# One block of scores per attention step, expert tiles in two phases, a prologue of two chains and the logits on GpSimd, in an attention and mixture-of-experts kernel on one core

## The reference, cut to what matters

```python
h = relu(patches(x, 5 frames) @ tok_W.T + tok_b)       # [32, 121, 128]
h = batch_norm(h) * gamma + beta                       # statistics over all 3872 rows
# attention in each sequence, with one bias per head and key column
xn = layernorm(h)
q, k, v = (xn @ w.T + b for each of q, k, v)           # heads of 16
scores = q @ k.T / 4 + col_bias                        # [32, 8, 121, 121]
h = h + softmax(scores) @ v @ o_w.T + o_b
# one expert per row
xf = layernorm(h)
expert = argmax(xf @ Wr + br)                          # top 1, its gate is 1
h = h + relu(xf @ W1[expert] + b1[expert]) @ W2[expert] + b2[expert]
```

## Time and profile before

| stretch of the profiled execution | us | what happens |
|---|---|---|
| 0 to 43.9 | 43.9 | prologue, up to the first scores |
| 43.9 to 206.8 | 162.9 | the starts of steps 0 to 31 |
| 206.8 to 242.5 | 35.7 | step 31, emptying, the table of tiles, first load |
| 242.5 to 313.6 | 71.1 | 38 expert tiles on PE |
| 313.6 to 326.6 | 13.0 | last rows out, end of the program |

### The profile page before, as it was taken

How to read it: one execution, slowest core, us unless ns; L and a number is a source line. 1 busy time by engine, 2 the same in 40 slices (tenths; PEclk the granted TensorE clock), 3 DMA queues, 4 the chain that set the end, 5 groups by cost and what they waited for, 6 DMA issues and landing times.

```text
span 326.6 us, 9082 instructions
## 1 busy us (share of the span) xinstructions
PE 256.3 (78%) x2851; PEld 211.5 (65%) x2851; DVE 193.1 (59%) x754; ACT 165.2 (51%) x427; POOL 140.7 (43%) x256
## 2 busy tenths in 40 slices
PE   3896577988898887789788978674149999999970
PEld 3765455765676665666556757442139999999970
DVE  3796325656766766757667657744716556656640
ACT  3761145655545555465555443421027777777730
POOL 7002621233426644564556363355603445545550
PEclk9995579999979999889999799955559999999996
DMA  3200698000000001001010101112133333333300
GB/s 99 67 2 0 197 314 252 3 2 0 3 17 17 25 25 33 17 18 33 15 34 17 33 16 36 31 32 57 56 87 90 94 104 117 93 107 101 87 11 0
DMA packets 15373, 19.13 MB, mean 59 GB/s; under 512 B 4007, under 2 KB 11467, under 8 KB 15328
## 3 DMA queue, kind: packets, MB, share of 16 engines
q1 hardware_dynamic: 11888, 12.15, 13.3%
q0 software_dynamic: 3296, 6.00, 6.2%
q10 hardware_dynamic: 144, 0.41, 0.4%
HBM read 10.58 MB, written 8.47 MB: 58 GB/s over the span
## 4 chain that ended last, share of the span: by engine, by line
PE 41%; issue 23%; POOL 20%; DVE 7%; ACT 4%; DMA 1%; POOLq 1%; SPq 1%; DVEq 0%; ACTq 0%
PE psS L1091 11%; POOL region_d L375 6%; PE psO L1102 5%; PE psU L1102 5%; POOL rs L347 3%; POOL rs L369 3%; PE psU L1028 2%; PE psS L928 2%; DVE sq L640 2%; PE psB L912 2%; ACT PT L492 2%; POOL var L364 2%; PE psU L1038 2%; POOL rows L358 2%; POOL xn L353 1%
## 5 line engine op out<-in xcount | busy, mean ns | idle before, releaser
L728 DVE TENSOR_REDUCE nmax<-psS 121x4 f32<-121x484 f32 x64 | 41.5, 660 | 41.7 <-PE psS L938 21.5
L403 POOL DMA_INDIRECT out<-y_out,sidx x38 | 36.9, 972 | 45.8 <-DVE y_out L832 42.2
L841 DVE TENSOR_SCALAR hT<-psS,b1T 128x128 f32<-128x128 f32 x76 | 23.3, 346 | 34.3 <-PE psS L1091 34.0
L1091 PE MATMUL psS<-xgT,W_tile 128*128 128x128 f32 x304 | 41.9, 283 | 0.0
L375 POOL DMA_INDIRECT region_d<-rows,pos x32 | 34.7, 1083 | 9.5 <-issue 8.7
L1091 PEld LDWEIGHTS psS<-xgT,W_tile 128*128 128x128 f32 x304 | 38.6, 199 | 0.0
L484 ACT ACTIVATE rows<-rows,rs 121x128 f32<-121x128 f32 x32 | 12.9, 402 | 48.1 <-POOL rs L369 48.0
L1028 PE MATMUL psU<-owX,oT 128*121 128x137 f32 x64 | 16.6, 344 | 21.3 <-ACT oT L495 21.3
L928 PE MATMUL psS<-kT,qT 32*121 32x121 f32 x512 | 23.7, 301 | 10.6 <-DVE kT L666 8.6
L541 ACT ACTIVATE hT<-psS,b1T 128x128 f32<-128x128 f32 x76 | 23.8, 364 | 14.1 <-PE psS L1091 14.0
L928 PEld LDWEIGHTS psS<-kT,qT 32*121 32x121 f32 x512 | 18.0, 190 | 18.9 <-issue 18.9
(11 more groups left out here) (223 smaller groups left out, 608.3 us busy)
## 6 DMA issues: line engine op xcount, KB each, us to landing
xg<-region_d SPq DMA_DIRECT2D x38, 129.0 KB, 2.1
W_sb<-in_L_ffn_W SPq DMA_DIRECT2D x1, 2048.0 KB, 9.2
region_d<-pads SPq DMA_DIRECT2D x1, 1032.0 KB, 7.0
region_d<-pads SPq DMA_DIRECT2D x1, 903.0 KB, 9.1
out<-y_out,sidx POOLq DMA_INDIRECT x38, 2.2
...
region_d<-rows,pos POOLq DMA_INDIRECT x32
...
```

Of the source, the lines that this page charges most:

```text
L403: pool.indirect_dma_start(out, bass.IndirectOffsetOnAxis(sidx[:, s:s + 1], 0), y_out[:, u, :], None, bounds_check=N - 1, oob_is_err=False) ...
L728: dve.tensor_reduce(nmax[0:L, pair * 64:pair * 64 + 64].rearrange("p (j c) -> p j c", c=HB)[:, :, HD + 1:HD + 3], score_half(0, pair), AX. ...
L841: ins = dve.tensor_scalar(hT[:, s % 2, c * 128:(c + 1) * 128], psS[:, 2 + s % 2, c % 2 * 128:(c % 2 + 1) * 128], b1T[:, bass.ds(e * FC + c ...
L1091: ins = pe.matmul(psS[:, c // 2 * 2 + s % 2, c % 2 * 128:(c % 2 + 1) * 128], W1_tile[:, s % 2, c * 128:(c + 1) * 128], xgT[:, s % 2, :], s ...
```

## The change

- **One block per step.** `nmax` is one instruction over all four banks, and so is the exponent. The order in a step is now maxima of t first, and then the exponent of t - 1, which waits for them.
- **Order of the queues.** On ACT the copy of the turned result (`turned_copy`) stands at the front of a step, and the scaling of the rows of t - 5 (`scaled_rows`) at its end. On DVE K's copy stands ahead of `qm`. On PE the output multiplication no longer has an exponent ahead of the ACT copy that it waits for.
- **Logits on Pool.** Instead of one DVE instruction per sequence, POOL does two instructions for each group of four. `rs2` has eight slots, so the wait on the scaling of b - 4 becomes one on b - 8.
- **Groups.** All groups have four sequences (8 groups). Their row bases are carried in `seen`, which takes one matmul out of each ranking.
- **Two phases of tiles.** After five groups (`EARLY`, sequences 0 to 19) the rows are counted in step 27 (`COUNT`), and the first NT1 = 11 full tiles are placed by step 29. SP loads them as soon as the rows of 20 sequences have landed. Their processing starts in the emptying: steps 32 to 36 each hold one tile (`ALONG` = 5). Tiles 5 to 10 follow, while DVE works out the table of the remaining NT2 = 27 tiles, one tile slot per partition. These 27 follow as before. In the first phase the output of W2 goes to one buffer in `psB` and not to two. The ring of row buffers has 12 instead of 8 places.
- **Prologue.** The identity matrix is made first, and PE starts on the patches with only that and `xs`. The one-hot rows are 64 `tensor_scalar` instructions of 121 columns, all ahead of the `bn_stats`. Half of their matmuls stand ahead of the frame multiplication, and half behind. ACT makes the copies of the weights and the first squares. K of the first pair is projected before the bias is turned, and Q after it. The third pair's turning stands behind these projections, and the second pair's norm is turned inside step 0.

The diff, cut to its core:

```diff
-RING = 8
+RING = 12
-XT = NT - -(-N // 128)
+EARLY = 5
-GROUPS = tuple((b, 4) for b in range(0, B - 8, 4)) + tuple((b, 2) for b in range(B - 8, B, 2))
+GROUPS = tuple((b, 4) for b in range(0, B, 4))
+B1 = GROUPS[EARLY - 1][0] + GROUPS[EARLY - 1][1]
+NT1 = (B1 * L - E * 127 + 127) // 128
+NT2 = NT - NT1
-        STEPS = B + 6
+        STEPS = B + 5
-            return b0 + nb + 5
+            return b0 + nb + (5 if b0 + nb <= B - 8 else 6 if b0 + nb < B else 4)
+        COUNT = ranked(EARLY - 1) + 2
+        ALONG = STEPS - B
...
-            sp.wait_ge(d_rows, 16 * B)
-            sp.wait_ge(d_pads, 32)
             sp.wait_ge(r_row, 1)
-            for s in range(NT):
+            first = first_row(0)
+            sp.wait_ge(d_early, 16 * B1)
+            sp.wait_ge(d_pads, 16)
+            load_rows(0, first)
+            for s in range(1, NT1):
+                load_rows(s, first_row(s))
+            sp.wait_ge(r_row, 2)
+            first = first_row(NT1)
+            sp.wait_ge(d_rows, 16 * (B - B1))
...
+            def logits(g):
...
+                pool.wait_ge(s_r2, b0 + nb)
+                pool.tensor_tensor(lg[0:L, v:v + nb, :], rows[0:L, b0:b0 + nb, 0:E],
+                                   rs2[0:L, v:v + nb].unsqueeze(2).to_broadcast([L, nb, E]), ALU.mult).then_inc(s_lg, 1)
+                pool.wait_ge(s_lg, 2 * g + 1)
+                pool.tensor_tensor(lg[0:L, v:v + nb, :], lg[0:L, v:v + nb, :],
+                                   br_bc[0:L, :].unsqueeze(1).to_broadcast([L, nb, E]), ALU.add).then_inc(s_lg, 1)
...
+            def exponent(b):
+
+                act.wait_ge(s_ST, b + 1)
+                if b + 1 < B:
+                    act.wait_ge(s_max, b + 2)
+                if b >= 2:
+                    act.wait_ge(s_PV, b - 1)
+                act.activation(PT[0:L, b % 2, :, :, :], score_half(1), ACT.Exp).then_inc(s_exp, 1)
...
-                dve.tensor_tensor(target1h[:, 8 * c:8 * c + 8, :],
-                                  slot_iota[:, 1:L + 1].unsqueeze(1).to_broadcast([128, 8, L]),
-                                  keyT[:, 8 * c:8 * c + 8].unsqueeze(2).to_broadcast([128, 8, L]),
-                                  ALU.is_equal).then_inc(a_1h, 1)
+            for c in range(8):
+                for f in range(8 * c, 8 * c + 8):
+                    ins = dve.tensor_scalar(target1h[:, f, :], slot_iota[:, 1:L + 1], keyT[:, f:f + 1], None, ALU.is_equal)
+                ins.then_inc(a_1h, 1)
...
-                    for pair in range(2):
-                        if pair == 1 and t > 0:
-                            dve.wait_ge(s_exp, 2 * t - 1)
-                        dve.tensor_reduce(nmax[0:L, pair * 64:pair * 64 + 64].rearrange("p (j c) -> p j c", c=HB)[:, :, HD + 1:HD + 3],
-                                          score_half(0, pair), AX.X, ALU.max, negate=True).then_inc(s_max, 1)
+                dve.tensor_reduce(nmax[0:L, :].rearrange("p (j c) -> p j c", c=HB)[:, :, HD + 1:HD + 3], score_half(0),
+                                  AX.X, ALU.max, negate=True).then_inc(s_max, 1)
...
+            for t in range(B + 1, STEPS):
+                s = t - B
+                e = tile_expert(s - 1)
...
+                if has(t, 3):
+                    turn_back(t - 3)
...
+                if has(t, 4):
+                    output(t - 4)
+                if has(t, 2):
+                    weigh(t - 2)
+                pe.wait_ge(f_xT, s + 1)
+                transpose_rows(s + 1)
+                ffn_first(s)
...
+                    turn(t - 3)
...
+                ffn_second(s - 1, e)
```

979 lines of the change are left out of this document (601 added, 378 removed).

## The result

The changed kernel takes **266.48 us** (median of four runs from 264.37 to 267.29), beside 327.67 us for the kernel before on the same chip: ratio 0.8119, 95% interval 0.8067 to 0.817. The profiled execution took 264.37 us by its own time, with a span of 262.6 us.

A forecast was written before the change was run, and what follows sets the result against it. PE was taken to bound the experts, latency the emptying, and a ring of waits to cost the nearly PE-full attention steps 0.82 us each. Gains of 17 + 5.5 + 16 = 38.5 us gave 289 us, range 277 to 303.

The forecast's parts named there:

- That is 4.43 us of work in a step of 5.25 us: Attention steps before the change: PE busy 137.4 of 162.9 us over 31 step starts, its busy time taken as work.
- The forecast of 4.7: Attention steps: the time in us taken for one step after the change, down from 5.25.
- The 5.0: Attention steps: upper bound in us of a step, if only the `oT` wait goes and a third of it returns.
- The ring: Attention steps: DVE's squares, POOL's root, ACT's scaling, exponent, DVE's second maxima; said to lose PE 0.82 us a step.
- part 1: Attention steps: reordered queues shorten 31 steps from 5.25 to 4.70 us, gaining 17 us, between 8 and 25.
- The cover of 3.0 us: Attention steps: PE work between one `scores_T` and the next scores, said to hide 2.5 us of maxima and exponent.
- PE full: Rival, attention steps: steps come down to 4.45 us, part 1 gives 25 us, time 281 us; chance 0.2.
- Another wait takes its place: Rival, attention steps: maxima or K's copy hold steps at 5.0 us, part 1 gives 8, time 298 us; chance 0.2.
- POOL becomes the bound: Rival, attention steps: the logits stretch POOL until steps exceed 5.95 us and the kernel is slower; chance 0.02.
- Part 2, 5.5 us: Prologue: statistics 2 us sooner, PE's earlier start 0.5, fetch to first scores 3; gain 5.5 us, between 3 and 7.
- Part 3: Emptying and experts: tiles begun in the emptying and a second phase gain 16 us, between 10 and 21.
- The tail: Program end: last row scatter starts 4.4 us after PE's end and 8.6 us follow, expected unchanged.

## Why the prediction was off

**The step that failed: "That is 4.43 us of work in a step of 5.25 us".** PE's busy time was taken for its work, and so for the least that a step can take. It is not work alone. The trace of before has one even step without a wait, step 4, the last one without a scaling. Here it is beside a step with the clock low and the two steps of the earlier trace rows (columns of the earlier trace rows):

```profile
60.81:65.17 4.36, 4.36 (x67) 3.60 (x67) 2.91 (x13) 2.77 (x8) 0.39 (x2) 1.00 0.02 6
92.51:98.44 5.93, 5.93 (x66) 5.03 (x66) 3.63 (x17) 2.75 (x8) 2.25 (x5) 0.71 0.09 24
148.51:153.72 5.21, 4.81 (x67) 3.64 (x67) 3.65 (x17) 2.95 (x9) 2.24 (x5) 1.00 0.10 28
153.72:159.79 6.07, 4.47 (x67) 3.33 (x67) 4.61 (x19) 3.25 (x9) 3.81 (x7) 1.00 0.08 21
```

The same 67 matmuls at the same clock are busy for 4.36 us without waits and for 4.81 with them. A matmul is recorded with 0.26 to 0.29 us, though in a block the next one starts 0.03 us later, so the first tenths of a stop do not show as idle. Step 20 has an example:

```profile
151.36 0.49 PE L1028 MATMUL psU<-owX,oT 128*121 128x137 f32 x2 [0.36 <-ACT oT L495]
151.90 0.32 PE L1038 MATMUL psU<-ident,nmax 121*128 121x121 f32 x1
```

The second maxima end at 151.84, and PE's turning of them starts at 151.90, 0.54 us after the block ahead of it, where 0.24 is enough in the timeline of the changed kernel. No idle time stands there. The steps 20 and 21 hold 9.29 us of busy time; an even step and an odd one with a ranking take PE 4.34 + 3.93 = 8.27 us now (with one bf16 matmul fewer). The least could thus have been read from the trace of before: 4.36 us in step 4, or from start to start of PE's blocks wherever no wait stands. In the changed kernel's timeline the ten gaps are 0.53, 0.53, 0.16, 0.22, 0.44, 0.46, 0.24, 0.19, 0.56 and 1.01 us, or 4.34. The clock has a small part too: the three even steps of before with a granted clock of 0.71 to 0.72 took 5.93, 5.87 and 5.30 us where the others took 5.0 to 5.2, some 1.5 us together, all booked as busy, and the changed kernel has none of them.

The forecast of 4.7, chosen between 4.43 and 5.0, was thus between two numbers that were both too high. The 5.0 does not follow from its own terms either: 5.25 less two thirds of 0.69 is 4.8.

**The ring was read rightly in the main.** The two moves that the first paragraph of part 1 names, scaling and K's copy, make 32.1 of the 37.6 us in the kernel before. But "the exponent no longer waits for POOL" was only half of it. With the maxima in one piece, the copy to `oT` is the edge that costs (13.0 us if it is behind the scaling, 0.5 if only the exponent is). The cover of 3.0 us of PE's work for maxima and exponent was enough: ACT waits 15.2 us for `nmax`, and PE hardly at all for ACT.

**The rivals.** "PE full" (0.2) was what happened, priced at 4.45 us a step and 281 us; with 4.04 its sum would be 281 - 31 x 0.41 = 268. So the rival had the mechanism and shared the wrong price. "Another wait takes its place" and "POOL becomes the bound" did not come: POOL is busy 77.64 of 125.3 us, 2.5 us a step. The signs given for part 1 (starts 4.6 to 4.8 us apart) were wrong in the size, and PE's wait for `oT` below 5 us was right (1.3).

**Logits on POOL, and the skill.** On the same 121x32 columns POOL takes 0.24 and 0.25 us and DVE 0.19. The rule of the Trainium skill ("GPSIMD Engine Reference", section "Engine selection") that such work is about twice as fast on VectorE is true in its direction, with 1.3 for these two-input operations; and since DVE's time is nearer the path, the move that the rule speaks against gains up to 0.9 us. The lock of the shared ports (the Trainium skill, "SBUF — State Buffer", section "SBUF: two separate sides") left no mark in the stage, and no run isolates it.

**Part 2, 5.5 us, was right in the sum, with some luck,** since the usual gain is nearer 4.8 (see the table of stages). The 64 short one-hots took 10.38 us (9 taken, between 7.3 and 14.5), 0.16 us from start to start though each is recorded with 0.25. The estimates from the Trainium skill ("VectorE: DVE Perf Modes", sections "The perf-mode tier table" and "The TRN2 errata") were 5.9 us at four columns a cycle and 11.9 at one; the 10.38 us of the trace are nearer the second. The statistics end at 23.23 instead of 24.98, the fetch starts at 29.26 instead of 31.61, and from there to the scores it is 9.1 instead of 12.3 us: 1.75 + 0.6 + 3.2 us against 2 + 0.5 + 3.

**Part 3, 19.3 instead of 16 us, was right to tile 11.** The W1 block of tile 11 was forecast 4.7 + 20 + 11.2 + 2.5 = 38.4 us behind the last scores and came at 38.1. Two small errors cancel in this: that of tile 5 came at 23.2 instead of 24.7, and the six tiles behind it took 14.9 instead of 13.7. The mixed tiles start 3.2, 4.3, 3.9, 2.5 and 2.9 us apart, the first one 6.5 us after the last scores. The gap for the second table is ahead of tile 8 and not at tile 11:

```profile
190.93 1.06 PE L1222 MATMUL psS<-xgT,W_tile 128*128 128x128 f32 x8
193.06 0.18 PE L1404 MATMUL psU<-ident,place 27*1 27x27 f32 x1 [1.07 <-DVE place L1024]
193.60 0.18 PE L1406 MATMUL psU<-ident,place 27*1 27x27 f32 x1 [0.36 <-DVE again L1029]
195.55 1.06 PE L1222 MATMUL psS<-xgT,W_tile 128*128 128x128 f32 x8
```

4.6 us instead of 1.9, so 2.7 where 2.5 were set. The miss is in the mark of the end. 313.6 us in the table of before is about the start of the last tile's W1 block (313.47). The sum after tile 11 counted 27 tiles and half of one more to get there, 51.4 us, where 26 tiles do, which took 49.3. On top of it 1 us was taken off the gain for the single buffer, of which the end shows nothing.

**The tail was put at "as before"** and is 1.6 us shorter, 1.35 of them by the waits that now stand on SP. That move is in the change and was overlooked in the forecast.
